# One of two transpose copies and the row sums go from ScalarE to VectorE (gated attention and a two-layer local-attention block on 8 cores)

## The chip, the cores and the metric

The kernel runs on all 8 cores of one Trainium2 chip. Each core takes one batch element (2048 x 1024) and all weights; the cores exchange nothing. The time is device microseconds of the slowest core. A core's engines are called PE (TensorE), ACT (ScalarE), DVE (VectorE), POOL (GpSimd) and SP (SyncE).

## The reference, cut to what matters

```python
xn = layernorm(x)
# gated attention; its softmax runs over the features D
q, k = silu(normed @ W_qk + b_qk) * gamma[0] + beta[0], ... * gamma[1] + beta[1]
sim  = einsum('bid,biD->bdD', q, k) / seq_len
attn = softmax(sim, axis=-1)
out  = v * sum(attn, axis=-1)[:, None, :]      # a row sum of a softmax
s    = (out * gate) @ W_out + b_out + xn
# two layers of local attention (8 heads of 64, window 512, one window back) and FFN
sim  = einsum('bhwid,bhwjd->bhwij', bq, bk)    # masked to a band of 512 back
attn = softmax(sim, axis=-1)
o    = einsum('bhwij,bhwjd->bhwid', attn, bv)
x    = x + o @ wo ;  x = x + ffn(x)
return x0 + s * silu(x)
```

## The kernel before

The program is a list of tasks written in order. `Prog.task` puts a task at the end of its engine's queue and works out from the names it reads and writes which semaphores it waits for; an engine runs its queue strictly in the order in which the tasks were written. `flush` closes a stage: all engines meet there, and the next stage's loads and products start behind it. The stages are: transposed layer norm, the QK projection, the similarity stage (`attn_p2`), the gated values and output (`attn_p34`), then for each of two layers QKV, local attention (`_local_attn`), the output projection, layer norm and FFN, and at last the final product.

**Similarity stage** (`attn_p2`, lines 563 to 644). The 2048 rows of `sim` are made in 16 blocks of 128 (`dt`), two for each of 8 query tiles `QT2` (called QT in the trace). For a query tile DVE makes 16 pieces with two instructions each (L588, L593). For a block PE makes 64 products of 512 columns into one half of `psim` (L605), DVE takes the row maximum (L614) and scales it (L618), ACT takes the exponential into `EB` with its sum in `small` (L623), DVE takes the reciprocal of this sum (L629), and ACT passes over `EB` once more, scaled by the reciprocal, with the sum of the result as `rowsum` (L633). Nothing but the sum is read later. In DVE's queue the next query tile stands behind the reciprocal of the pair's second block.

**Local attention** (`_local_attn`, from L1301). Two heads are worked on together (u = 0 and 1, the halves of the partitions), in 4 pairs `hp`, 4 windows `w` of 512 queries, and 4 steps `it` of 128 queries: 16 windows and 64 steps per layer. In a window w > 0 a step sees a band of 640 keys ("full band"), in w = 0 of 128, 256, 384 and 512. A step is:
- scores into `pS[u]` (L1329) and on top of them the mask as a product with the identity (L1336), for both u;
- then, of the step before, the transposes of `PB` into `pPT[u]` (L1396), and the copy of `pPT[u]` to `PT` (L1404, on ACT), both u;
- the softmax: negated row maxima of both u (L1350, DVE), exponentials of both u from `pS` into `PB` with their sums (L1358, ACT), reciprocals (L1367, DVE), and the scaling of `PB` (L1374, DVE).

The scores of the next step write `pS[u]`, so they wait for this step's exponential of the same u. Behind the fourth step come its own transposes and copies, and then the output product over all of `PT` (L1440), which ACT moves to `OA` (L1450). The order is the one of this loop:

```python
for it in range(4):
    for u in range(2):
        s_task(hp, w, it, u, jt0, iv)
    if it > 0:
        emit_tp(hp, w, it - 1)
    softmax(hp, w, it)
emit_tp(hp, w, 3)
```

`pPT` has a bank of PSUM for each u, and `pS` two. For V, DVE copies transposes out of a bf16 PSUM tile in the QKV stage (L865, `tensor_copy`).

Of the kernel before, what the change touches and what calls it, by code (L numbers as in the profile page):

```python
# [9 lines left out]
BF16 = mybir.dt.bfloat16  # L10
AF = mybir.ActivationFunctionType
ALU = mybir.AluOpType
# [5 lines left out]
HIDDEN, QKD = 2048, 2048  # L18
# [236 lines left out]
class Build:  # L255
# [307 lines left out]
    def attn_p2(self):  # L563
        nc, p, h = self.nc, self.p, self.h
        QK, GBC = self.QK, self.GBC
        gbc_res = tuple(f"GBC{r}.{c}" for r in range(4) for c in range(4))
        small = self.small
        with ExitStack() as S2:
            KF = S2.enter_context(nc.sbuf_tensor("KF", [128, NT, QKD], BF16))
            QT2 = S2.enter_context(nc.sbuf_tensor("QT2", [128, 2, NT, 256], BF16))  # L570
            EB = S2.enter_context(nc.sbuf_tensor("EB", [128, 2, QKD], BF16))
            psim = S2.enter_context(nc.psum_tensor("psim", [128, 2, QKD], F32))

            for t in range(NT):
                p.task("vector", lambda e, t=t: e.tensor_tensor(
                    KF[:, t, :], QK[:, t, :], GBC[:, 2, :], op=ALU.mult),
                    reads=(f"QK{t}.0", f"QK{t}.1", f"QK{t}.2", f"QK{t}.3")
                    + gbc_res,
                    writes=(f"KF{t}",), tag=f"p2.km{t}")
                p.task("vector", lambda e, t=t: e.tensor_tensor(  # L580
                    KF[:, t, :], KF[:, t, :], GBC[:, 3, :], op=ALU.add),
                    reads=(f"KF{t}",), writes=(f"KF{t}",), tag=f"p2.ka{t}")
            kf_res = tuple(f"KF{t}" for t in range(NT))

            for dp in range(8):
                qp = dp % 2
                for kt in range(NT):
                    p.task("vector", lambda e, dp=dp, kt=kt, qp=qp: e.tensor_tensor(  # L588
                        QT2[:, qp, kt, :], QK[:, kt, dp * 256:(dp + 1) * 256],
                        GBC[:, 0, dp * 256:(dp + 1) * 256], op=ALU.mult),  # L590
                        reads=(f"QK{kt}.{dp // 2}",) + gbc_res,
                        writes=(f"QT2{qp}.{kt}",), tag=f"p2.qm{dp}.{kt}")
                    p.task("vector", lambda e, dp=dp, kt=kt, qp=qp: e.tensor_tensor(  # L593
                        QT2[:, qp, kt, :], QT2[:, qp, kt, :],
                        GBC[:, 1, dp * 256:(dp + 1) * 256], op=ALU.add),
                        reads=(f"QT2{qp}.{kt}",), writes=(f"QT2{qp}.{kt}",),
                        tag=f"p2.qa{dp}.{kt}")
                qt_res = tuple(f"QT2{qp}.{kt}" for kt in range(NT))
                for dt in range(dp * 2, dp * 2 + 2):
                    pb = dt % 2  # L600
                    dl = (dt % 2) * 128
                    def simmm(e, dt=dt, pb=pb, dl=dl, qp=qp):
                        for c in range(4):
                            for kt in range(NT):
                                mm = e.matmul(  # L605
                                    psim[:, pb, c * 512:(c + 1) * 512],
                                    QT2[:, qp, kt, dl:dl + 128],
                                    KF[:, kt, c * 512:(c + 1) * 512],
                                    start=(kt == 0), stop=(kt == NT - 1))
                        return mm  # L610
                    p.task("tensor", simmm, reads=qt_res + kf_res,
                           writes=(f"psim{pb}",), tag=f"p2.sim{dt}")
                    sb = pb * 4
                    p.task("vector", lambda e, pb=pb, sb=sb: e.tensor_reduce(  # L614
                        small[:, sb:sb + 1], psim[:, pb, :], axis=AX.X, op=ALU.max),
                        reads=(f"psim{pb}",), writes=(f"p2max{pb}",),
                        tag=f"p2.max{dt}")
                    p.task("vector", lambda e, sb=sb: e.tensor_scalar(  # L618
                        small[:, sb + 1:sb + 2], small[:, sb:sb + 1], -1.0 / N,
                        None, op0=ALU.mult),  # L620
                        reads=(f"p2max{pb}",), writes=(f"p2bias{pb}",),
                        tag=f"p2.b{dt}")
                    p.task("scalar", lambda e, pb=pb, sb=sb: e.activation(  # L623
                        EB[:, pb, :], psim[:, pb, :], AF.Exp,
                        bias=small[:, sb + 1:sb + 2], scale=1.0 / N,
                        accum_out=small[:, sb + 2:sb + 3]),
                        reads=(f"psim{pb}", f"p2bias{pb}"),
                        writes=(f"EB{pb}", f"p2z{pb}"), tag=f"p2.exp{dt}")
                    p.task("vector", lambda e, sb=sb: e.reciprocal(  # L629
                        small[:, sb + 3:sb + 4], small[:, sb + 2:sb + 3]),  # L630
                        reads=(f"p2z{pb}",), writes=(f"p2rz{pb}",),
                        tag=f"p2.rz{dt}")
                    p.task("scalar", lambda e, dt=dt, pb=pb, sb=sb: e.activation(  # L633
                        EB[:, pb, :], EB[:, pb, :], AF.Identity,
                        scale=small[:, sb + 3:sb + 4],
                        accum_out=self.rowsum[:, dt:dt + 1]),
                        reads=(f"EB{pb}", f"p2rz{pb}"),
                        writes=(f"EB{pb}", f"rowsum{dt}"), tag=f"p2.rs{dt}")
            if "dbg_rowsum" in self.dbg_h:
                p.dma("sync", self.dbg_h["dbg_rowsum"][:], self.rowsum[:],  # L640
                      reads=tuple(f"rowsum{dt}" for dt in range(NT)),
                      writes=("dbg_rowsum.0",), tag="dbg.rowsum")
                self.out_res.append("dbg_rowsum.0")
            p.flush("p2")
# [656 lines left out]
    def _local_attn(self, l, QP, KP, VTM, OA, PB, PT, pS, pPT, pO):  # L1301
        p = self.p
        small = self.small
# [4 lines left out]
        def band(w, it):  # L1308
            if w == 0:
                return 0, (it + 1) * 128  # L1310
            return it * 128, 640
# [76 lines left out]
        def emit_tp(hp, w, it):  # L1388
            jlo, W = band(w, it)
            jb0 = jlo // 128  # L1390
            nb = W // 128
            for u in range(2):
                def ptp(e, u=u, it=it, jb0=jb0, nb=nb):
                    for jj in range(nb):
                        jb = jb0 + jj
                        mm = e.transpose(  # L1396
                            pPT[:, u, jj * 128:(jj + 1) * 128],
                            PB[:, it % 2, u, jb * 128:(jb + 1) * 128],
                            self.ident_bf[:])
                    return mm  # L1400
                p.task("tensor", ptp, reads=(f"PB{u}.{it % 2}", "identity_bf"),
                       writes=(f"pPT{u}",), tag=f"f{l}.tp{hp}.{w}.{it}.{u}")
                def pev(e, u=u, it=it, jb0=jb0, nb=nb):
                    return e.activation(  # L1404
                        PT[:, u, jb0:jb0 + nb, it * 128:(it + 1) * 128],
                        pPT[:, u, 0:nb * 128].rearrange("p (a b) -> p a b", b=128),
                        AF.Identity)
                p.task("scalar", pev, reads=(f"pPT{u}",),
                       writes=(f"PTc{u}.{it}",),
                       tag=f"f{l}.pe{hp}.{w}.{it}.{u}")  # L1410

        def icols(w, jt, njt):
            if w == 0:
# [5 lines left out]
        for hp in range(4):  # L1419
            for w in range(NW):  # L1420
                jt0 = 0 if w == 0 else (w - 1) * 4
                njt = 4 if w == 0 else 8
                for it in range(4):
                    iv = w * 512 + it * 128
# [6 lines that stand above are left out]
                pt_res = tuple(f"PTc{u}.{it}" for u in range(2) for it in range(4))  # L1431
                pbo = w % 2
                jt_order = list(range(njt)) if w == 0 else [3, 4, 2, 5, 1, 6, 0, 7]
                def omm(e, hp=hp, w=w, jt0=jt0, pbo=pbo, jt_order=jt_order):
                    for u in range(2):
# [13 lines left out]
                       writes=(f"pO{pbo}",), tag=f"f{l}.O{hp}.{w}")  # L1449
# [3 lines left out]
                    reads=(f"pO{pbo}",), writes=(f"OA{hp}.{w}",),  # L1453
                    tag=f"f{l}.Oe{hp}.{w}")
# [73 lines left out]
```

How the kernel before makes its waits and increments, by code:

```python
                    def _(eng):  # L114
                        cov = self.cov[e]
                        for (deps, emit, dslot, tag) in tasks:
                            for key, val in sorted(deps.items()):
                                if cov.get(key, 0) >= val:
                                    continue
                                if key[0] == "d":
                                    sem = self.dsems[key[1]][key[2]]
                                else:
                                    sem = self.sems[key[1]]
                                eng.wait_ge(sem, val)
                                cov[key] = val
                            if emit is None:
                                continue
                            if dslot is not None:
                                insts = emit(eng)
                                assert len(insts) == 1, tag
                                insts[0].then_inc(self.dsems[e][dslot], 16)
                            else:
                                inst = emit(eng)
                                if inst is None:
                                    inst = eng.nop()
                                inst.then_inc(self.sems[e], 1)
```

## Time and profile before

| | us |
|---|---|
| median of 2 runs | 4052.85 |
| the two runs | 3993.53 and 4112.18 |
| the profiled execution | 4013.77 |
| its span on the slowest core (core 1) | 4012.1 |
| spans of the other cores | 3970.2 to 3998.7 |

Busy over the span: PE 2726.5 us (68%), DVE 1149.4 (29%), ACT 916.6 (23%), POOL 203.9 (5%). Local attention of layer 0 lies at about 1537 to 1898 us, that of layer 1 at 2880 to 3236, the similarity stage at 442 to 791. The rows further down are of three kinds: groups of instructions with their mean duration and the idle time ahead of them; the timeline, where each row is a run of like instructions on one engine, with the idle time of the engine ahead of it and who ended it in brackets; and busy time by stage. In the timeline the start comes first and then the length, which for "x2" is from the first's start to the second's end.

### The profile page before, as it was taken

Reading aid. Unit: us, or ns where it says so; the run is one execution under the profiler, and the core shown is the slowest. Engines: PE = TensorE matmul, PEld = TensorE weight load, DVE = VectorE, ACT = ScalarE, POOL = GpSimd, SP = SyncE. Lnnn points to the kernel's source line nnn. Section 1 sums busy time; section 2 is a strip of 40 time slices with the busy share of each in tenths; the row PEclk is TensorE's granted clock in tenths of the full one; section 3 lists DMA queues with packets and bytes.
Section 4 is the critical chain, followed back from the end, with each engine's and each line's share of the span. In section 5 each row is a group of like instructions: output and inputs, shape, how many; then the busy total and the mean of one; then the engine's idle time right before and its main releaser. Section 6 shows DMA issues by size and latency. Waiting matters only on the chain. (4 is left out here: it accounts for less than half of the span.)

```text
span 4012.1 us, 34877 instructions; the slowest of 8 cores (3970.2 to 4012.1 us)
## 1 busy us (share of the span) xinstructions
PE 2726.5 (68%) x11952; PEld 1166.5 (29%) x11952; DVE 1149.4 (29%) x2109; ACT 916.6 (23%) x1570; POOL 203.9 (5%) x262
## 2 busy tenths in 40 slices
PE   1289476559693556655679898855665656989982
PEld 1223132224241113333123333311233322433432
DVE  3510523201012344443511111234444353111113
ACT  2322022123211213454021011021245412101101
POOL 0000000000000000000010111100000000111110
PEclk8577788879896766555789999966655577999995
DMA  5200000040344100000045555501000003565557
GB/s 125 80 6 1 0 0 0 15 70 1 58 130 128 21 11 11 1 1 5 7 53 63 58 68 62 65 11 21 11 1 1 1 11 37 69 61 60 63 59 251
DMA packets 213603, 170.26 MB, mean 42 GB/s; under 512 B 97573, under 2 KB 193976, under 8 KB 208312
## 3 DMA queue, kind: packets, MB, share of 16 engines
q0 software_dynamic: 200896, 119.59, 21.2%
q1 hardware_dynamic: 12536, 48.44, 4.1%
q8 instruction: 101, 1.65, 0.2%
q14 instruction: 70, 0.57, 0.1%
HBM read 237.26 MB, written 25.17 MB: 65 GB/s over the span
## 5 line engine op out<-in xcount | busy, mean ns | idle before, releaser
L1208 PE MATMUL pa<-N,W1B 128*128 128x512 bf16 x1408 | 339.1, 384 | 68.7 <-DMA W1B<-w1ag 68.7
L1170 PE MATMUL px<-PROD,W2B 128*128 128x512 bf16 x1408 | 324.0, 387 | 49.2 <-DMA W2B<-w2cb 49.0
L605 PE MATMUL psim<-KF,QT 128*128 128x512 bf16 x1024 | 236.2, 395 | 154.5 <-DVE QT L593 154.5
L1220 PE MATMUL pg<-N,W1B 128*128 128x512 bf16 x1408 | 336.2, 382 | 0.0
L1232 DVE TENSOR_TENSOR PROD<-pa,GEB 128x1024 bf16<-128x1024 f32 x88 | 107.8, 1225 | 630.9 <-ACT GEB L1227 630.9
L1329 PE MATMUL pS<-KP,QP 64*128 64x512 bf16 (+2 forms) x448 | 153.3, 426 | 162.1 <-ACT PB L1358 129.2
L889 PE MATMUL pqkv<-ABF,WQKV 128*128 128x512 bf16 x768 | 204.3, 432 | 64.8 <-DVE ESC L836 47.7
L1350 DVE TENSOR_REDUCE small<-pS 128x1 f32<-128x640 f32 (+4 forms) x256 | 183.3, 737 | 189.8 <-PE pS L1336 185.0
L1227 ACT ACTIVATE GEB<-pg,B1G 128x1024 bf16<-128x1024 f32 x88 | 98.1, 1115 | 553.9 <-PE pg L1220 553.9
L1396 PE MATMUL pPT<-ident_bf,PB 128*128 128x128 bf16 x1120 | 144.2, 311 | 99.1 <-DVE PB L1374 99.1
L1208 PEld LDWEIGHTS pa<-N,W1B 128*128 128x128 bf16 x1408 | 138.4, 99 | 240.1 <-issue 79.3
L1404 ACT ACTIVATE PT<-pPT 128x640 bf16<-128x640 bf16 (+4 forms) x256 | 149.8, 635 | 229.7 <-PE pPT L1396 229.2
L1170 PEld LDWEIGHTS px<-PROD,W2B 128*128 128x128 bf16 x1408 | 134.8, 99 | 222.8 <-issue 76.9
L1358 ACT ACTIVATE PB<-pS,small 128x640 bf16<-128x640 f32 (+4 forms) x256 | 184.8, 734 | 30.3 <-PE pS L1336 16.3
L605 PEld LDWEIGHTS psim<-KF,QT 128*128 128x128 bf16 x1024 | 102.9, 101 | 287.6 <-issue 176.6
L1220 PEld LDWEIGHTS pg<-N,W1B 128*128 128x128 bf16 x1408 | 123.6, 98 | 166.6 <-issue 43.1
L670 PE MATMUL pv<-ABF,WH 128*128 128x512 bf16 x512 | 122.5, 383 | 63.0 <-DMA WH<-W_hidden 63.0
L1396 PEld LDWEIGHTS pPT<-ident_bf,PB 128*128 128x128 bf16 x1120 | 120.2, 147 | 106.9 <-issue 106.6
L544 PE MATMUL pqk<-WQK,ABF 128*128 128x512 bf16 x512 | 147.5, 441 | 0.0
L1183 DVE TENSOR_TENSOR XF<-XF,px 128x512 f32<-128x512 f32 x64 | 44.0, 688 | 338.5 <-PE px L1173 338.5
L736 PE MATMUL ps<-VG,WO 128*128 128x512 bf16 x512 | 112.8, 384 | 39.0 <-DMA WO<-W_out 39.0
L889 PEld LDWEIGHTS pqkv<-ABF,WQKV 128*128 128x128 bf16 x768 | 82.8, 109 | 182.9 <-issue 117.6
(140 smaller groups left out, 2822.0 us busy)
## 6 DMA issues: line engine op xcount, KB each, us to landing
W1B<-w1ag POOLq DMA_DIRECT2D x88, 512.0 KB, 6.0
W2B<-w2cb POOLq DMA_DIRECT2D x32, 704.0 KB, 8.3
XT<-x SPq DMA_DIRECT2D x16, 512.0 KB, 4.2
xn_scr<-XNW POOLq DMA_DIRECT2D x16, 512.0 KB, 3.8
WH<-W_hidden POOLq DMA_DIRECT2D x8, 1024.0 KB, 32.0
XNB<-xn_scr SPq DMA_DIRECT2D x8, 1024.0 KB, 6.5
s_scr<-SB POOLq DMA_DIRECT2D x8, 1024.0 KB, 8.6
XF<-xn_scr SPq DMA_DIRECT2D x8, 1024.0 KB, 23.6
```

Source lines behind the costliest of these rows:

```text
L544: e.matmul(pqk[:, pb, :], ABF[:, k, t * 128:(t + 1) * 128], WQK[:, k, c * 512:(c + 1) * 512], start=(k == 0), stop=False)
L605: mm = e.matmul(psim[:, pb, c * 512:(c + 1) * 512], QT2[:, qp, kt, dl:dl + 128], KF[:, kt, c * 512:(c + 1) * 512], start=(kt == 0), stop=( ...
L670: mm = e.matmul(pv[:, sc, :], WH[:, k, hp * 128:(hp + 1) * 128], ABF[:, k, c * 512:(c + 1) * 512], start=(k == 0), stop=(k == DT - 1))
L889: mm = e.matmul(pqkv[:, sc, :], WQKV[:, k, ms * 128:(ms + 1) * 128], ABF[:, k, c * 512:(c + 1) * 512], start=(k == 0), stop=(k == DT - 1))
L1170: e.matmul(px[:, pb, :], W2B[:, s2, k, :], PROD[:, k, cc * 512:(cc + 1) * 512], start=(k == 0), stop=False)
L1208: e.matmul(pa[:, mp, cc * 512:(cc + 1) * 512], W1B[:, sl, k, 0:128], self.N2[:, k, nh0 + cc * 512:nh0 + (cc + 1) * 512], start=(k == 0), s ...
L1220: mm = e.matmul(pg2[:, mp, cc * 512:(cc + 1) * 512], W1B[:, sl, k, 128:256], self.N2[:, k, nh0 + cc * 512:nh0 + (cc + 1) * 512], start=(k ...
L1329: e.matmul(pS[:, u, lo:lo + n], QP[u * 64:(u + 1) * 64, hp, iv:iv + 128], KP[u * 64:(u + 1) * 64, hp, jt0 * 128 + lo:jt0 * 128 + lo + n], ...
L1350: p.task("vector", lambda e, u=u, sc=sc, jlo=jlo, W=W: e.tensor_reduce(small[:, sc:sc + 1], pS[:, u, jlo:jlo + W], axis=AX.X, op=ALU.max, ...
L1358: e.activation(PB[:, it % 2, u, jlo:jlo + W], pS[:, u, jlo:jlo + W], AF.Exp, bias=small[:, sc:sc + 1], accum_out=small[:, sc + 1:sc + 2]),
L1396: mm = e.transpose(pPT[:, u, jj * 128:(jj + 1) * 128], PB[:, it % 2, u, jb * 128:(jb + 1) * 128], self.ident_bf[:])
L1404: return e.activation(PT[:, u, jb0:jb0 + nb, it * 128:(it + 1) * 128], pPT[:, u, 0:nb * 128].rearrange("p (a b) -> p a b", b=128), AF.Iden ...
```

## The change

In the similarity stage the second pass of ACT over `EB` goes; in its place DVE multiplies the sum by its reciprocal, one number a partition. `EB` is now one tile and not two. In local attention the copy of u = 1 out of `pPT` is a `tensor_scalar` with 1.0 on DVE; the copy of u = 0 stays on ACT. The copies stay where they stood in the program, in `emit_tp`.

```diff
-            EB = S2.enter_context(nc.sbuf_tensor("EB", [128, 2, QKD], BF16))
+            EB = S2.enter_context(nc.sbuf_tensor("EB", [128, QKD], BF16))
...
-                    p.task("scalar", lambda e, dt=dt, pb=pb, sb=sb: e.activation(
-                        EB[:, pb, :], EB[:, pb, :], AF.Identity,
-                        scale=small[:, sb + 3:sb + 4],
-                        accum_out=self.rowsum[:, dt:dt + 1]),
-                        reads=(f"EB{pb}", f"p2rz{pb}"),
-                        writes=(f"EB{pb}", f"rowsum{dt}"), tag=f"p2.rs{dt}")
+                    p.task("vector", lambda e, dt=dt, sb=sb: e.tensor_tensor(
+                        self.rowsum[:, dt:dt + 1], small[:, sb + 2:sb + 3],
+                        small[:, sb + 3:sb + 4], op=ALU.mult),
+                        reads=(f"p2z{pb}", f"p2rz{pb}"),
+                        writes=(f"rowsum{dt}",), tag=f"p2.rs{dt}")
...
+                if u == 0:
...
+                    p.task("scalar", pev, reads=(f"pPT{u}",),
...
+                else:
+                    def pev(e, u=u, it=it, jb0=jb0, nb=nb):
+                        return e.tensor_scalar(
+                            PT[:, u, jb0:jb0 + nb, it * 128:(it + 1) * 128],
+                            pPT[:, u, 0:nb * 128].rearrange("p (a b) -> p a b",
+                                                            b=128),
+                            1.0, None, op0=ALU.mult)
+                    p.task("vector", pev, reads=(f"pPT{u}",),
+                           writes=(f"PTc{u}.{it}",),
+                           tag=f"f{l}.pe{hp}.{w}.{it}.{u}")
```

DVE's queue in local attention, full-band windows of layer 0, before (L1350 maxima, L1367 reciprocals, L1374 scaling of `PB`; "waits" names the semaphores that an instruction waits for):

```order
L1350 TENSOR_REDUCE small<-pS 128x1 [waits sem_tensor] x2
L1367 RECIPROCAL small<-small 128x1 [waits sem_scalar] x2
L1374 TENSOR_SCALAR PB<-PB,small 128x640 [waits sem_vector] x2
L1350 TENSOR_REDUCE small<-pS 128x1 [waits sem_tensor] x2
L1367 RECIPROCAL small<-small 128x1 [waits sem_scalar] x2
L1374 TENSOR_SCALAR PB<-PB,small 128x640 [waits sem_vector] x2
```

And now, from the start of a window (the lines are one less than before up to here, and L1414 is the copy of u = 1):

```order
L1349 TENSOR_REDUCE small<-pS 128x1 [waits sem_tensor] x2
L1366 RECIPROCAL small<-small 128x1 [waits sem_scalar] x2
L1373 TENSOR_SCALAR PB<-PB,small 128x640 [waits sem_vector] x2
L1414 TENSOR_SCALAR PT<-pPT 128x5x128 [waits sem_tensor]
L1349 TENSOR_REDUCE small<-pS 128x1 x2
L1366 RECIPROCAL small<-small 128x1 [waits sem_scalar] x2
L1373 TENSOR_SCALAR PB<-PB,small 128x640 [waits sem_vector] x2
L1414 TENSOR_SCALAR PT<-pPT 128x5x128 [waits sem_tensor]
```

A copy stands between the scaling of one step and the maxima of the next. It waits for PE; the maxima behind it have no wait of their own left, since the transposes stand behind their scores on PE.

DVE's queue in the similarity stage, before, where a pair of blocks ends and the next query tile begins:

```order
L618 TENSOR_SCALAR small<-small 128x1 [waits sem_vector]
L629 RECIPROCAL small<-small 128x1 [waits sem_scalar]
L588 TENSOR_TENSOR QT<-QK,GBC 128x256
L593 TENSOR_TENSOR QT<-QT,GBC 128x256 [waits sem_vector]
L588 TENSOR_TENSOR QT<-QK,GBC 128x256
```

And now:

```order
L618 TENSOR_SCALAR small<-small 128x1 [waits sem_vector]
L629 RECIPROCAL small<-small 128x1 [waits sem_scalar]
L633 TENSOR_TENSOR rowsum<-small 128x1 [waits sem_vector]
L588 TENSOR_TENSOR QT<-QK,GBC 128x256
L593 TENSOR_TENSOR QT<-QT,GBC 128x256 [waits sem_vector]
```

The row sum (L633) stands between the reciprocal and the next query tile, and waits for the reciprocal.

## Rows read from the trace of the kernel before

**Rows 1.** The page, its first line

```profile
span 4012.1 us, 34877 instructions; the slowest of 8 cores (3970.2 to 4012.1 us)
```

**Rows 2.** Busy time by stage (from:to, length, busy us per engine, granted clock)

```profile
1537.00:1898.00 361.00, 217.72 (x1220) 114.79 (x1221) 146.10 (x384) 178.59 (x400) 0.00 (x0) 0.53 0.01 3
...
442.00:791.00 349.00, 236.19 (x1024) 102.93 (x1024) 97.25 (x273) 67.76 (x65) 0.18 (x1) 0.85 0.00 0
```

**Rows 3.** Groups of instructions, shapes apart (| busy us, mean ns | idle before, releaser)

```profile
L1350 DVE TENSOR_REDUCE small<-pS 128x1 f32<-128x640 f32 x192 | 152.2, 820 | 142.5 <-PE pS L1336 140.2 <-issue 0.6
...
L1440 PE MATMUL pO<-PT,VTM 128*64 128x512 bf16 x112 | 55.4, 626 | 31.6 <-ACT PT L1404 31.6
```

**Rows 4.** Timeline, one step of a full-band window (start us, us, engine line)

```profile
1611.74 0.69 PE L1329 MATMUL pS<-KP,QP 64*128 64x256 bf16 x2 [1.89 <-ACT PB L1358]
...
1613.07 1.59 DVE L1350 TENSOR_REDUCE small<-pS 128x1 f32<-128x640 f32 x2
...
1613.52 1.27 PE L1396 MATMUL pPT<-ident_bf,PB 128*128 128x128 bf16 x10
...
1614.35 1.30 ACT L1404 ACTIVATE PT<-pPT 128x640 bf16<-128x640 bf16 x2 [2.09 <-PE pPT L1396]
...
1615.54 0.80 ACT L1358 ACTIVATE PB<-pS,small 128x640 bf16<-128x640 f32 x1
...
1616.68 0.69 PE L1329 MATMUL pS<-KP,QP 64*128 64x128 bf16 x2 [1.89 <-ACT PB L1358]
```

**Rows 5.** Timeline, first step of another window

```profile
1644.87 0.40 PE L1336 MATMUL pS<-MSK,ident_bf 128*128 128x128 bf16 x2
...
1645.37 1.80 DVE L1350 TENSOR_REDUCE small<-pS 128x1 f32<-128x640 f32 x2 [4.16 <-PE pS L1336]
...
1646.29 0.80 ACT L1358 ACTIVATE PB<-pS,small 128x640 bf16<-128x640 f32 x1 [1.30 <-PE pS L1336]
```

**Rows 6.** Groups of instructions of DVE, shapes apart, and one pair in the timeline

```profile
L1350 DVE TENSOR_REDUCE small<-pS 128x1 f32<-128x384 f32 x16 | 8.9, 555 | 0.8
...
L865 DVE COPY VTM<-ptv 128x512 bf16<-128x512 bf16 x32 | 12.0, 417 | 3.4 <-PE ptv L855 3.4
...
L1374 DVE TENSOR_SCALAR PB<-PB,small 128x640 bf16<-128x640 bf16 x192 | 65.6, 383 | 0.8 <-DVE small L1367 0.6
...
1512.98 0.74 DVE L865 COPY VTM<-ptv 128x512 bf16<-128x512 bf16 x2
```

**Rows 7.** Timeline, end of a full-band window

```profile
1622.89 1.23 PE L1396 MATMUL pPT<-ident_bf,PB 128*128 128x128 bf16 x10 [3.15 <-DVE PB L1374]
...
1623.68 1.30 ACT L1404 ACTIVATE PT<-pPT 128x640 bf16<-128x640 bf16 x2 [1.52 <-PE pPT L1396]
...
1625.12 3.81 PE L1440 MATMUL pO<-PT,VTM 128*64 128x512 bf16 x16 [1.01 <-ACT PT L1404]
```

**Rows 8.** Timeline, middle step of a first window (w = 0)

```profile
1634.21 0.63 PE L1396 MATMUL pPT<-ident_bf,PB 128*128 128x128 bf16 x4
...
1635.27 0.59 ACT L1358 ACTIVATE PB<-pS,small 128x384 bf16<-128x384 f32 x1
```

**Rows 9.** Timeline, similarity stage, a pair of blocks and the stage ends

```profile
521.41 0.16 DVE L629 RECIPROCAL small<-small 128x1 f32<-128x1 f32 x1 [2.25 <-ACT EB L623]
...
521.49 0.27 DVE L588 TENSOR_TENSOR QT<-QK,GBC 128x256 bf16<-128x256 bf16 x1
...
521.87 0.29 DVE L593 TENSOR_TENSOR QT<-QT,GBC 128x256 bf16<-128x256 bf16 x1
...
788.00 2.00 ACT L633 ACTIVATE EB<-EB,small 128x2048 bf16<-128x2048 bf16 x1 [0.36 <-DVE small L629]
...
789.90 0.19 ACT L633 ACTIVATION_READ_ACCUMULATOR EB<-EB,small 128x1 f32 x1
...
790.82 4.29 POOL L94 DMA_DIRECT2D WH<-W_hidden  x8 [578.63 <-SPq L106]
```

**Rows 10.** Timeline, output product of another full-band window

```profile
1600.75 3.29 PE L1440 MATMUL pO<-PT,VTM 128*64 128x512 bf16 x16 [1.01 <-ACT PT L1404]
```

More of the change, by code:

```diff
@@ L623, in attn_p2 @@
                     p.task("scalar", lambda e, pb=pb, sb=sb: e.activation(
-                        EB[:, pb, :], psim[:, pb, :], AF.Exp,
+                        EB[:, :], psim[:, pb, :], AF.Exp,
                         bias=small[:, sb + 1:sb + 2], scale=1.0 / N,
@@ L627, in attn_p2 @@
                         reads=(f"psim{pb}", f"p2bias{pb}"),
-                        writes=(f"EB{pb}", f"p2z{pb}"), tag=f"p2.exp{dt}")
+                        writes=("EB0", f"p2z{pb}"), tag=f"p2.exp{dt}")
                     p.task("vector", lambda e, sb=sb: e.reciprocal(
@@ L1402, in emit_tp, with pev @@
                        writes=(f"pPT{u}",), tag=f"f{l}.tp{hp}.{w}.{it}.{u}")
[L1403 to L1410, printed above, removed]
+                if u == 0:
+                    def pev(e, u=u, it=it, jb0=jb0, nb=nb):
+                        return e.activation(
+                            PT[:, u, jb0:jb0 + nb, it * 128:(it + 1) * 128],
+                            pPT[:, u, 0:nb * 128].rearrange("p (a b) -> p a b",
+                                                            b=128),
+                            AF.Identity)
+                    p.task("scalar", pev, reads=(f"pPT{u}",),
+                           writes=(f"PTc{u}.{it}",),
+                           tag=f"f{l}.pe{hp}.{w}.{it}.{u}")
+                else:
+                    def pev(e, u=u, it=it, jb0=jb0, nb=nb):
+                        return e.tensor_scalar(
+                            PT[:, u, jb0:jb0 + nb, it * 128:(it + 1) * 128],
+                            pPT[:, u, 0:nb * 128].rearrange("p (a b) -> p a b",
+                                                            b=128),
+                            1.0, None, op0=ALU.mult)
+                    p.task("vector", pev, reads=(f"pPT{u}",),
+                           writes=(f"PTc{u}.{it}",),
+                           tag=f"f{l}.pe{hp}.{w}.{it}.{u}")
         def icols(w, jt, njt):
```

## The prediction, made before the changed kernel ran

> **What bounds the kernel now.** I began with the span [rows 1]: 4012.1 us on the slowest core in an execution of 4013.77 us, so 1.7 us lie around it. The sum below is made against 4013.77. The median of the two runs shown is 4052.85 us, 1% above it, and the two lie 119 us apart (3993.53 and 4112.18); a time near the upper one would have to be read with that in mind.
>
> Then busy time by stage [rows 2]. The diff touches the similarity stage once (about 349 us) and the local attention of both layers (about 360 us each). In local attention no engine is full: PE is busy 218 of 361 us, DVE 146, ACT 179, at a granted clock of 0.53, which is near the lower of the two levels (1.2 GHz). A stage in which nothing is full and the clock is low is bound by a chain of waits that goes round between engines. So what counts is not how much work an engine has, but what stands in front of the instruction that the chain passes through.
>
> The groups [rows 3] say where the waits are: DVE waits 142.5 us ahead of the row maxima (L1350), almost all for PE; the output product (L1440) waits 31.6 us for ACT's copies of the transposes (L1404), about 1 us in each of the 32 windows.
>
> The timeline of one step of the loop over `it` [rows 4] shows the round. At 1611.74 PE starts the scores of the next step, goes on with their mask products, and then transposes ten blocks of the present step, until 1613.52 + 1.27 = 1614.79. Meanwhile DVE has scaled PB and taken both maxima, 1613.07 to 1614.66, before the transposes are even done. ACT copies both halves (u=0, u=1) from 1614.35, and both exponentials come right behind: the first at 1615.54. The next scores can start only when it has emptied its half of pS: at 1616.68. One round is 4.94 us, and from the first exponential to the next scores are 1.14 us of it. The maxima are not on this round: they are over nearly a microsecond before the exponential starts.
>
> **Local attention: the copy of u=1 goes from ACT to DVE.** 128 copies leave ACT and 128 `tensor_scalar` come to DVE; 96 on each side have 640 columns. By work alone this is a gain: ACT is on the round, and it gets rid of one copy of some 0.65 us.
>
> But the order on DVE (see the change above) puts the copy of step it-1 ahead of both maxima of step it. It waits for the last transpose, which PE issues behind the scores of step it. So the maxima, which now run before and beside the transposes, must wait for them, and behind the maxima stand both exponentials, and the next scores behind the first exponential. The wait is long and its place is on the round. The new start of the first exponential is:
> - end of the transposes, 1614.79 [rows 4];
> - to the start of DVE's copy 0.10: a step's first mask products end at 1644.87 + 0.40 = 1645.27 and the maximum starts at 1645.37 [rows 5];
> - from the copy's start to the maximum's, d (below);
> - from the maximum's start to the exponential's 0.92, as 1645.37 to 1646.29, where nothing else held it [rows 5].
>
> With d = 0 this is already 1615.81, 0.27 later than the 1615.54 of today. Three such steps are 0.81 us, and all that a window's end can give back is less (0.76, below), so by this working there is no gain whatever the copy's speed.
>
> **The size of d.** The trace has no `tensor_scalar` from a bf16 tile in PSUM. Nearest is L865, DVE's copy from a bf16 PSUM tile in blocks of 128 with the same form of output: 417 ns for 512 columns, and two in 0.74 us, so 0.74 - 0.42 = 0.32 from start to start [rows 6]. The f32 maximum of L1350 takes 820 ns for 640 and 555 for 384 columns, 1.04 ns a column [rows 3, 6]; L865 spends less than that, and half of it per column (0.52) adds 0.07 for the other 128. So d = 0.39 and the copy is 0.48 long. Below: L1374 scales 640 bf16 columns in SBUF in 0.38, and with an overlap of 0.08, between the maxima's and L865's, d = 0.30 [rows 6]. Above: the rate of the f32 maxima, which are 0.82 long, two in 1.59, so d = 0.77 [rows 3, 4]. I take 0.39, since L865 differs least.
>
> The Trainium skill, in "VectorE: DVE Perf Modes", section "Rules for kernel authors", tells one to accept 1x for elementwise work on a matmul's output; by that the upper end, 0.77, would be the value. L865 is against it here, with 417 ns for 512 columns; I keep it as a rival.
>
> **Per window.** With d = 0.39 the first exponential starts at 1614.79 + 0.10 + 0.39 + 0.92 = 1616.20, so 0.66 late. The second needs the second maximum, 0.77 behind the first, and ACT spaces the exponentials 0.83 apart anyway, so it isn't later than that. All of this enters the round: 4.94 becomes 5.60. It happens in steps 1, 2 and 3 of a window (in step 0 the maxima stand behind the previous window's last copy, but they have to wait for the scores behind the output product anyway): 3 x 0.66 = 1.98.
>
> At the window's end something comes back. The last transposes end at 1622.89 + 1.23 = 1624.12 and ACT's copies of both halves run 1623.68 to 1624.98; the output product starts at 1625.12 [rows 7]. Now the halves run side by side, and DVE's ends at 1624.12 + 0.10 + 0.48 = 1624.70: 0.28 earlier (a copy of no length would give 1624.98 - 1624.22 = 0.76). Net 1.98 - 0.28 = 1.70 us in each of the 24 windows of full band: 40.8.
>
> The 8 first windows (w = 0) have bands of 128 to 512 columns. Middle step: transposes end 1634.21 + 0.63 = 1634.84, a copy of 256 columns gives d = 0.19 by the same rate, and the maximum of 384 columns to its exponential takes 0.55 + 0.10, so 1635.78 against 1635.27: 0.51 late [rows 8]. Three such and 0.2 back at the end (my estimate, from the 0.28 of a full band): 1.3 x 8 = 10.6. Both together: +51.4 us.
>
> With d = 0.30: 3 x 0.57 less 0.38 at the end = 1.33 x 24 = 32, and with 10 for the first windows +42. With d = 0.77: 3 x 1.04, and at the end DVE is 0.06 later than ACT was, so 3.18 x 24 = 76; the first windows' steps rise by some 0.18 each and lose their 0.2, so 2.1 x 8 = 17: +93.
>
> **Similarity stage: the row sum.** ACT's 16 passes over EB (2.0 us each) go; 16 products of 128x1 come to DVE. ACT is busy 68 of 349 us there [rows 2], and no instruction of the trace waits for these passes. Fifteen of the passes lie beside score products or DVE's query tiles, so removing them gives nothing. Only the last counts, as its accumulator is read at 789.90 + 0.19 = 790.09 and the next stage's weight loads leave behind it, at 790.82 [rows 9]. Its successor on DVE starts 0.11 behind the reciprocal (a dependent pair of DVE: 521.49 + 0.27 to 521.87), at 788.01, and is over by about 788.2: 1.9 us gained. Against that, the query tiles start 0.08 behind the reciprocal's start today (521.41 to 521.49) [rows 9] and PE waits for them; now a dependent product stands between, 0.16 + 0.11 = 0.27 more, in 7 places: 1.9 lost. Net 0; bounds -2 (nothing lost) and +2 (0.5 a place). The smaller EB frees room that nothing uses.
>
> **Sum.** 4013.8 + 51.4 + 0 = 4065, so +1.3%. A measurement of this kernel can tell about 2% (80 us) from no change; by this the forecast is "within 2%", on the slow side of it.
>
> **Rivals.**
> - *The copy runs at the rate of the f32 maxima* (d = 0.77): 4013.8 + 93 = 4107, slower by 2.3%. This is the case on the other side of the mark; the place is the wait of L1350 in the 96 steps; it decides when the copy of 640 columns takes over 0.74 us (42 us come with 0.38 more of d, so the 80 us are reached at d = 0.65). For it: the f32 reads of PSUM in rows 3 and 6 run so. Against: L865.
> - *The clock.* The output product of a full-band window takes 3.29 us or 3.81 [rows 7, 10]; I read this as the clock going to its upper level earlier or later in it. If PE, idler now, lost this in all 24 windows, and the scores behind it lost as much again (my estimate), 24 x 2 x 0.52 = 25 us would come on top: 4090, 1.9%. For it: the clock is 0.53 already. Against: it rises during the output product, which doesn't change.
> - *The freed copy is what counts.* If the maxima weren't late, the exponential would start one copy earlier: 0.65 in 72 steps, half of that (my estimate) in the 24 narrow ones, and 8 us at the windows' ends, 63 in all: 3951, faster by 1.6%. The Trainium skill, "ScalarE: Activation LUTs", section "Rules for kernel authors", is for it: multiplications belong on VectorE rather than on ScalarE; the trace agrees as to length (L865 and L1404, 0.48 by my estimate against some 0.65). Against the rival is the order: the maxima can't pass the copy.
> - *Nothing moves*, 4014: the late exponentials would have to be paid by a wait between them and the next scores. The trace has no such wait in the 1.14 us that lie there.
>
> **Chances.** Forecast 0.70; f32 rate 0.13; clock 0.08; freed copy 0.04; nothing 0.05. The second lies over 2%, and half of the clock case, which is 4 us short of it: slower 0.17. Faster by 2% needs more than any case gives: 0.02; within: 0.81. The range: low end 4013.8 + 42, less the 20 us by which the faster run shown lies under the profiled one, 4036; high end the second case's 4107 and 20 for the same, 4127.
>
> **What would show it.** Right: in a full-band step L1350 starts behind DVE's copy and ACT waits ahead of L1358 for L1350's maximum; the round is 5.5 to 5.7 us; the copy row reads 0.45 to 0.50; local attention is 25 us longer per layer; the output product waits for ACT or DVE 0.7 us a window. The similarity stage keeps its length within 2 us. Wrong: a round of 4.94 or less, or exponentials that start right behind ACT's copy, or a copy row of 0.8.

## The result, and the profile after

The changed kernel is slower by 1.4%: the ratio is 1.0138, with a 95% interval of [1.0093, 1.0182]. Its median over 11 runs is 4060.16 us. The median of the kernel before over all its 10 runs is 4076.46 us, above this, because medians count disturbed executions too, which the ratio leaves out on both sides. The profiled execution took 4045.38 us, against 4013.77 before. The two profiles differ by less than 1.4%, since on the core that was the slowest before (and on one other) the score products of the similarity stage began some 25 us later than on most others (442.4 against about 416 us), ahead of everything that the change touches; stage lengths, further down, are free of this.

The page's first lines, core 2, the slowest:

```profile
span 4043.4 us, 34668 instructions; the slowest of 8 cores (4031.8 to 4043.5 us)
...
PE 2698.1 (67%) x11952; PEld 1162.5 (29%) x11952; DVE 1204.4 (30%) x2253; ACT 824.7 (20%) x1410; POOL 203.9 (5%) x262
```

ACT has lost 92 us of work and DVE has gained 55, and the kernel is longer. Busy time of local attention in layer 0 (from:to, length, busy us of PE, PEld, DVE, ACT and POOL, granted clock), as in [rows 2]; it takes 386 us where it took 361:

```profile
1512.00:1898.00 386.00, 216.04 (x1216) 113.86 (x1216) 171.95 (x448) 149.79 (x336) 0.00 (x0) 0.54 0.01 3
```

The groups, as in [rows 3] (busy us, mean ns, idle before and its releasers):

```profile
L1357 ACT ACTIVATE PB<-pS,small 128x640 bf16<-128x640 f32 x192 | 151.1, 791 | 114.8 <-DVE small L1349 96.1 <-PE pS L1335 16.9 <-DVE small L1366 0.5
L1349 DVE TENSOR_REDUCE small<-pS 128x1 f32<-128x640 f32 x192 | 149.8, 815 | 99.6 <-PE pS L1335 97.8
...
L1404 ACT ACTIVATE PT<-pPT 128x640 bf16<-128x640 bf16 x96 | 67.6, 704 | 181.1 <-PE pPT L1395 181.1
...
L1414 DVE TENSOR_SCALAR PT<-pPT 128x640 bf16<-128x640 bf16 x96 | 47.2, 491 | 147.9 <-PE pPT L1395 147.9
...
L1451 PE MATMUL pO<-PT,VTM 128*64 128x512 bf16 x112 | 55.4, 626 | 23.7 <-DVE PT L1414 23.7
```

DVE's reciprocals, before and after:

```profile
L1367 DVE RECIPROCAL small<-small 128x1 f32<-128x1 f32 x256 | 41.9, 164 | 237.2 <-ACT PB L1358 235.8
```

```profile
L1366 DVE RECIPROCAL small<-small 128x1 f32<-128x1 f32 x256 | 42.0, 164 | 118.8 <-ACT PB L1357 117.5
```

Three entries tell the story. Ahead of the exponentials (L1357) ACT now waits 96.1 us for DVE's maxima. The new copy (L1414) waits 147.9 us for the transposes. And DVE's wait for the exponentials, ahead of its reciprocals, has fallen from 237.2 to 118.8 us: where it used to take both maxima first and then wait, it now waits for the transposes first, and the maxima are late by it. The wait that stands in the row of the maxima itself (142.5 us before, 99.6 now) isn't the sign of the loss: 140.0 of the 142.5 us and 97.2 of the 99.6 lie in the first steps of the windows, ahead of the first maximum. The copy itself takes 491 ns.

One step of a full-band window in the timeline, the counterpart of [rows 4]:

```profile
1593.13 0.69 PE L1328 MATMUL pS<-KP,QP 64*128 64x256 bf16 x2 [2.56 <-ACT PB L1357]
...
1594.91 1.27 PE L1395 MATMUL pPT<-ident_bf,PB 128*128 128x128 bf16 x10
1595.75 0.70 ACT L1404 ACTIVATE PT<-pPT 128x640 bf16<-128x640 bf16 x1 [2.09 <-PE pPT L1395]
1596.30 0.49 DVE L1414 TENSOR_SCALAR PT<-pPT 128x640 bf16<-128x640 bf16 x1 [1.75 <-PE pPT L1395]
1596.70 1.54 DVE L1349 TENSOR_REDUCE small<-pS 128x1 f32<-128x640 f32 x2
1597.61 0.79 ACT L1357 ACTIVATE PB<-pS,small 128x640 bf16<-128x640 f32 x1 [1.16 <-DVE small L1349]
...
1598.75 0.69 PE L1328 MATMUL pS<-KP,QP 64*128 64x128 bf16 x2 [2.56 <-ACT PB L1357]
```

The round is 1598.75 - 1593.13 = 5.62 us, where it was 4.94. The reader should go down the starts: transposes end at 1594.91 + 1.27 = 1596.18, the copy starts 0.12 behind, the first maximum 0.40 behind that, the exponential 0.91 behind that, the next scores 1.14 behind that. ACT has been done with its own copy since 1596.45 and idles 1.16 us until the maximum is there.

The end of a window, as in [rows 7], with both copies side by side and PE's wait at 0.75 us, which was 1.01:

```profile
1605.86 1.22 PE L1395 MATMUL pPT<-ident_bf,PB 128*128 128x128 bf16 x10 [4.06 <-DVE PB L1373]
1606.65 0.70 ACT L1404 ACTIVATE PT<-pPT 128x640 bf16<-128x640 bf16 x1 [1.52 <-PE pPT L1395]
1607.19 0.49 DVE L1414 TENSOR_SCALAR PT<-pPT 128x640 bf16<-128x640 bf16 x1 [1.18 <-PE pPT L1395]
...
1607.83 3.81 PE L1451 MATMUL pO<-PT,VTM 128*64 128x512 bf16 x16 [0.75 <-DVE PT L1414]
```

The middle step of a first window, as in [rows 8]:

```profile
1520.13 0.63 PE L1395 MATMUL pPT<-ident_bf,PB 128*128 128x128 bf16 x4
...
1520.88 0.29 DVE L1414 TENSOR_SCALAR PT<-pPT 128x256 bf16<-128x256 bf16 x1 [1.10 <-PE pPT L1395]
...
1521.72 0.58 ACT L1357 ACTIVATE PB<-pS,small 128x384 bf16<-128x384 f32 x1 [0.69 <-DVE small L1349]
```

From the transposes' end (1520.76) to the exponential are 0.96 us, where it was 0.43. In the similarity stage, as in [rows 9], first a pair's end, then the stage's end, and last the reciprocal that began the stage's end in the kernel before:

```profile
495.94 0.16 DVE L629 RECIPROCAL small<-small 128x1 f32<-128x1 f32 x1 [2.25 <-ACT EB L623]
496.21 0.16 DVE L633 TENSOR_TENSOR rowsum<-small 128x1 f32<-128x1 f32 x1
496.29 0.29 DVE L588 TENSOR_TENSOR QT<-QK,GBC 128x256 bf16<-128x256 bf16 x1
```

```profile
762.77 0.16 DVE L629 RECIPROCAL small<-small 128x1 f32<-128x1 f32 x1 [2.25 <-ACT EB L623]
763.03 0.16 DVE L633 TENSOR_TENSOR rowsum<-small 128x1 f32<-128x1 f32 x1
763.94 4.29 POOL L94 DMA_DIRECT2D WH<-W_hidden  x8 [551.38 <-SPq L106]
```

```profile
787.74 0.16 DVE L629 RECIPROCAL small<-small 128x1 f32<-128x1 f32 x1 [2.26 <-ACT EB L623]
```

From the reciprocal's start to the query tile's are 0.35 us, which was 0.08; from the last reciprocal's start to the weight loads 1.17, which was 790.82 - 787.74 = 3.08.

A measure that the late start of two cores doesn't touch is the time from the first row maximum of layer 0 to the start of the last eviction of the output product of layer 1 on each core, with all that lies between. Its median over the eight cores is used below as "the attention stretch". It is 1690.1 us before and 1745.1 after: 55.0 us longer, 1.4% of the whole. The score products of the similarity stage, from the first start to the last and again as a median, take 341.1 us before and 341.6 after (339.0 to 341.8 on the single cores before).

### The profile page after: what moved, and what is told of

It reads as the page before. It is cut to its first block and busy times, and to the rows that moved or that the text cites. A ratio compares the mean times of both kernels' runs of the same rounds, so it can differ in the third digit from the quotient of the medians.

```text
span 4043.4 us, 34668 instructions; the slowest of 8 cores (4031.8 to 4043.5 us)
## 1 busy us (share of the span) xinstructions
PE 2698.1 (67%) x11952; PEld 1162.5 (29%) x11952; DVE 1204.4 (30%) x2253; ACT 824.7 (20%) x1410; POOL 203.9 (5%) x262
## 5 line engine op out<-in xcount | busy, mean ns | idle before, releaser
L1357 ACT ACTIVATE PB<-pS,small 128x640 bf16<-128x640 f32 (+4 forms) x256 | 184.1, 723 | 133.5 <-DVE small L1349 113.5
L669 PE MATMUL pv<-ABF,WH 128*128 128x512 bf16 x512 | 122.6, 383 | 61.3 <-DMA WH<-W_hidden 61.3
L735 PE MATMUL ps<-VG,WO 128*128 128x512 bf16 x512 | 112.2, 383 | 40.8 <-DMA WO<-W_out 40.8
L1404 ACT ACTIVATE PT<-pPT 128x640 bf16<-128x640 bf16 (+4 forms) x128 | 81.5, 637 | 226.9 <-PE pPT L1395 226.9
L460 PE MATMUL pbf<-ident_bf,NTB 128*128 128x128 bf16 x128 | 16.2, 305 | 160.3 <-DVE NTB L452 160.3
```

Source lines behind the costliest of these rows:

```text
L669: mm = e.matmul(pv[:, sc, :], WH[:, k, hp * 128:(hp + 1) * 128], ABF[:, k, c * 512:(c + 1) * 512], start=(k == 0), stop=(k == DT - 1))
L735: mm = e.matmul(ps[:, pb, :], WO[:, k, mo * 128:(mo + 1) * 128], VG[:, k, c * 512:(c + 1) * 512], start=(k == 0), stop=(k == NT - 1))
L1357: e.activation(PB[:, it % 2, u, jlo:jlo + W], pS[:, u, jlo:jlo + W], AF.Exp, bias=small[:, sc:sc + 1], accum_out=small[:, sc + 1:sc + 2]),
```

## The experiments

The order theory was: the copy stands in DVE's queue ahead of the next step's maxima, so the maxima wait for the transposes, and the exponentials and the next scores for the maxima. Its main rival, the work theory: DVE has more to do, or reads PSUM beside ACT, and that costs wherever the copy stands.

**The copy behind the maxima.** From the changed kernel, the put of the u = 1 copy is held back until `softmax` has written its two maxima:

```diff
-                        emit_tp(hp, w, it - 1)
-                    softmax(hp, w, it)
+                        held = emit_tp(hp, w, it - 1, late=(1,))
+                    softmax(hp, w, it, held_mx=held)
```

> The changed kernel with one thing moved: DVE's copy of u=1 stands behind the two maxima of the next step and no longer ahead of them. Order theory (the loss comes from what stands in front of the maxima, not from the work): the first exponential of a full-band step starts right behind ACT's single copy, about 0.59 us earlier than in the kernel before, the round falls from 4.94 to about 4.35 us, and with 0.28 at each window's end some 58 us are gained: 0.986 of the kernel before. Work theory (DVE has more to do and reads PSUM beside ACT, wherever the copy stands): the round stays at 5.6 us and the ratio at 1.014.

Measured: ratio 0.9837, interval [0.9813, 0.9861]; the attention stretch is 1628.8 us, 61.3 shorter than before the change and 116 shorter than after it. The timeline of a full-band step:

```profile
1587.23 0.70 ACT L1409 ACTIVATE PT<-pPT 128x640 bf16<-128x640 bf16 x1 [2.09 <-PE pPT L1400]
1587.78 0.49 DVE L1424 TENSOR_SCALAR PT<-pPT 128x640 bf16<-128x640 bf16 x1 [0.24 <-PE pPT L1400]
1587.83 0.79 ACT L1359 ACTIVATE PB<-pS,small 128x640 bf16<-128x640 f32 x1
...
1592.18 0.79 ACT L1359 ACTIVATE PB<-pS,small 128x640 bf16<-128x640 f32 x1
```

The same 0.49 us copy now runs beside the exponential (1587.78 and 1587.83), which starts right behind ACT's single copy. The next step's exponential is at 1592.18, 4.35 us after 1587.83, as expected. The work theory falls: DVE has the same 2253 instructions (busy 1206.5 us, against 1204.4), and the sign of the result has turned.

**The halves exchanged.** DVE copies u = 0, ACT u = 1, in the changed kernel's places.

```diff
-                if u == 0:
+                if u == 1:
                     def pev(e, u=u, it=it, jb0=jb0, nb=nb):
                         return e.activation(
```

> The changed kernel with the halves exchanged: the copy of u=0 is DVE's, that of u=1 is ACT's, same places in the order. DVE has the same work, but its transposes end 0.54 us earlier. Order theory: the maxima start that much earlier, the round is about 5.1 us (4.94 + 0.14), the loss falls to some 16 us, ratio about 1.004. Work theory: ratio 1.014 as before, round 5.6.

Measured: 1.0031 [1.0004, 1.0058]; attention stretch 1710.1, 20.0 longer than before, where some 16 were expected.

```profile
1591.82 0.69 PE L1328 MATMUL pS<-KP,QP 64*128 64x256 bf16 x2 [2.03 <-ACT PB L1357]
...
1594.45 0.49 DVE L1414 TENSOR_SCALAR PT<-pPT 128x640 bf16<-128x640 bf16 x1 [1.22 <-PE pPT L1395]
1594.86 1.55 DVE L1349 TENSOR_REDUCE small<-pS 128x1 f32<-128x640 f32 x2
...
1595.77 0.80 ACT L1357 ACTIVATE PB<-pS,small 128x640 bf16<-128x640 f32 x1
...
1596.91 0.69 PE L1328 MATMUL pS<-KP,QP 64*128 64x128 bf16 x2 [2.03 <-ACT PB L1357]
```

The round is 5.09 us. DVE's copy and maxima are where they were in the queue, but their transposes are ready earlier, and some two thirds of the loss are gone. What is paid is the moment at which the copy can start, plus its length.

**The copy twice.** A second `tensor_scalar` into the same place behind the first (the output doesn't change by it).

```diff
                     p.task("vector", pev, reads=(f"pPT{u}",),
                            writes=(f"PTc{u}.{it}",),
                            tag=f"f{l}.pe{hp}.{w}.{it}.{u}")
+                    p.task("vector", pev, reads=(f"pPT{u}",),
+                           writes=(f"PTc{u}.{it}",),
+                           tag=f"f{l}.pf{hp}.{w}.{it}.{u}")
```

> The changed kernel with DVE's copy made twice into the same place. The second waits for the first, so the maxima start 0.49 + 0.11 = 0.60 us later. Order theory (the copy's whole length is on the round): round 5.61 + 0.60 = 6.2 us, 43 us more in full-band steps, 10 in the narrow ones and 18 at the windows' ends, together 71 us more than the changed kernel, some 1.031 of the kernel before. If the length of the copy were hidden and only the wait for the transposes counted, the round would stay at 5.6.

This run gave no ratio, only the profile. The step on core 4:

```profile
1596.83 0.79 ACT L1357 ACTIVATE PB<-pS,small 128x640 bf16<-128x640 f32 x1 [1.76 <-DVE small L1349]
...
1601.12 1.09 DVE L1414 TENSOR_SCALAR PT<-pPT 128x640 bf16<-128x640 bf16 x2 [1.75 <-PE pPT L1395]
1602.13 1.55 DVE L1349 TENSOR_REDUCE small<-pS 128x1 f32<-128x640 f32 x2
1603.04 0.79 ACT L1357 ACTIVATE PB<-pS,small 128x640 bf16<-128x640 f32 x1 [1.76 <-DVE small L1349]
```

From the copy's start to the first maximum are 1.01 us, where one copy makes it 0.40: 0.61 more. The exponential is at 1603.04, against 1596.83 a step earlier: a round of 6.21. The attention stretch is 1817.6, 72.5 longer than after the change (1816.0 and 70.9 by cores 4 to 7 alone), where 71 were expected. So the copy's length stands on the round in full, and d, the term that the prediction had to bound, enters the sum as it had it.

**The row sum alone.** Local attention is that of the kernel before, the similarity stage that of the changed one.

```diff
-                    p.task("scalar", lambda e, dt=dt, pb=pb, sb=sb: e.activation(
...
+                    p.task("vector", lambda e, dt=dt, sb=sb: e.tensor_tensor(
+                        self.rowsum[:, dt:dt + 1], small[:, sb + 2:sb + 3],
+                        small[:, sb + 3:sb + 4], op=ALU.mult),
...
```

> The kernel before with only the row sum moved to DVE (similarity stage), local attention untouched. My theory: 1.9 us gained at the stage's end and 0.27 in each of 7 places lost, ratio 1.000 within the interval; the first to the last score product of the stage take 0.27 x 7 = 2 us longer, and the following stage starts 2 us sooner behind the last of them. Rival: the missing ACT passes free something that I haven't seen, ratio below 0.995.

> The kernel with only the row sum moved, once more and with more rounds, since the first time gave no interval. My theory: 1.000, within 0.002 either way. Rival: the row sum gives some of the time that the first run hinted at (its two lowest executions lay 5 us below those of the kernel before), ratio 0.998 or less.

Neither run gave a ratio. What they show: the lowest of the first was 3986.06 us and that of the second 3994.80, beside 3991.71 and 3991.46 for the kernel before on the same chip at the same time; one lies below and one above. The score products' stretch was 340.3 and 341.4 us (341.1 before), the attention stretch 1685.8 and 1687.4 (1690.1 before). These are differences that two profiles of one kernel could show as well. The row sum is worth less than these runs can tell, within some 6 us either way; that it is exactly nothing isn't shown.

**The copy alone.** The other half: similarity stage as before, local attention as changed.

```diff
+                else:
+                    def pev(e, u=u, it=it, jb0=jb0, nb=nb):
+                        return e.tensor_scalar(
...
+                    p.task("vector", pev, reads=(f"pPT{u}",),
```

> The kernel before with only the copy of u=1 moved to DVE, at the place that the change gives it. My theory: the whole loss, ratio 1.013 to 1.015, first maximum to last eviction of OA 55 us longer than in the kernel before. Rival: part of the loss comes from the row sum, ratio 1.010 or less.

Measured: 1.0109 [1.0055, 1.0163], an interval too wide to tell 1.010 from 1.014; one execution of the kernel before, at 4039.14, widens it. The lowest of each, 4043.07 and 3991.46, make 1.0129. The attention stretch decides it: 1742.9 us, 52.8 longer than before, against 55.0 with both parts. The loss is the copy's; the 2.2 us between the two are hardly more than the 1.6 by which the two profiles of the row-sum kernel differ.

**Both copies behind maxima and exponentials.** If the place in the queue is what counts, more can be moved out of the round's way: ACT's copy needn't stand ahead of the exponentials either.

```diff
-                        emit_tp(hp, w, it - 1)
-                    softmax(hp, w, it)
+                        held = emit_tp(hp, w, it - 1, late=(0, 1))
+                    softmax(hp, w, it, held_ex=held)
```

> The changed kernel with both copies of a step written behind the maxima and exponentials of the next step: ACT runs its exponentials ahead of its copy of u=0, DVE its maxima ahead of its copy of u=1. The round then no longer goes through transposes and copies: scores to first maximum 1.3 us (DVE has just scaled PB), to the exponential 0.92, to the next scores 1.14, together about 3.4 us against 4.35 with the copy only behind the maxima, with PE's 3.05 us of work per step close below. Order theory: 1.54 x 72 us and some 17 in the narrow steps and 8 at the windows' ends come off the kernel before, 0.966; somewhat less if PE's clock rises with its busier stage. Work theory: DVE with 3.2 us of work per step, and waits on PE's queue, keeps the round above 4 us: 0.98 or more.

Measured: 0.9698 [0.967, 0.9726], median 3870.14 us; attention stretch 1567.4, 122.7 shorter than before.

```profile
1576.86 0.79 ACT L1359 ACTIVATE PB<-pS,small 128x640 bf16<-128x640 f32 x1 [1.12 <-DVE small L1349]
...
1578.42 0.70 ACT L1409 ACTIVATE PT<-pPT 128x640 bf16<-128x640 bf16 x1
...
1579.33 1.59 DVE L1349 TENSOR_REDUCE small<-pS 128x1 f32<-128x640 f32 x2
...
1579.78 1.27 PE L1400 MATMUL pPT<-ident_bf,PB 128*128 128x128 bf16 x10
1580.24 0.80 ACT L1359 ACTIVATE PB<-pS,small 128x640 bf16<-128x640 f32 x1 [1.12 <-DVE small L1349]
```

The exponential starts 0.91 us behind the maximum and 0.81 us ahead of the end of the transposes of the step before (1581.05). From 1576.86, the exponential one step earlier, to 1580.24 are 3.38 us, as expected. The stretch became 123 us shorter, where I had worked out 136. The first windows gave the 17 us expected (16.5); the full-band ones gave 107.6 of 119, and where the other 11 are wasn't traced.

**The same order with all copies on ACT.** The kernel before, not the changed one, with the same two lines.

> The kernel before (both copies on ACT, second pass over EB on ACT) with only the order changed: both copies of a step behind the maxima and exponentials of the next. Order theory: ACT's 3.0 us of work per step fit into a round of about 3.4 us, so nearly all of the gain comes without moving any work to DVE: 0.97. If it is the split of the copies that makes the gain and order only lets it through, the round stays above 4.3 us: 0.985 or more.

Measured: 0.9703 [0.9675, 0.9732], median 3873.66 us; attention stretch 1567.0.

```profile
1575.77 0.80 ACT L1360 ACTIVATE PB<-pS,small 128x640 bf16<-128x640 f32 x1 [0.53 <-DVE small L1350]
...
1577.32 1.30 ACT L1409 ACTIVATE PT<-pPT 128x640 bf16<-128x640 bf16 x2
...
1578.68 1.27 PE L1401 MATMUL pPT<-ident_bf,PB 128*128 128x128 bf16 x10
1579.15 0.80 ACT L1360 ACTIVATE PB<-pS,small 128x640 bf16<-128x640 f32 x1 [0.53 <-DVE small L1350]
```

ACT makes both copies (1.30 us) between one step's exponentials and the next, and the round is 1579.15 - 1575.77 = 3.38 us, the same as with the split. With the order right, moving a copy to DVE is worth nothing that can be told: 0.9703 and 0.9698. With the order as it was, the move costs 1.4%. (The split kernel has the row sum on DVE too, this one on ACT; the attention stretch leaves that stage out.) Both these kernels beat the kernel before by 3% and the changed one by more than 4%.

## Why the prediction was right, and where it was wrong

**The round.** Right in each link. Forecast and measured: to DVE's copy 0.10 and 0.12; d 0.39 and 0.40; maximum to exponential 0.92 and 0.91; round 5.60 and 5.62. The experiment with the copy twice shows that d counts in full, and the one with the copy behind the maxima that nothing but its place makes the loss.

**The size of d.** L865 was the right row to go by: the copy takes 491 ns where 0.48 us was taken. The Trainium skill's "VectorE: DVE Perf Modes", section "Why PSUM operands drop a tier", caps an operand in PSUM at 2x, and an fp32 one at 1x; the rows agree, as 128 more columns cost 67 ns from 512 (424 ns) to 640 (491 ns), half of the 1.04 ns a column of the f32 maxima. The rule for authors that I weighed in the forecast, to accept 1x, doesn't hold for this source, and the rival of a copy at the f32 rate (d = 0.77) is out.

**The windows.** A window's end gave back 0.26 (PE's wait 1.01 to 0.75) of the forecast 0.28. The narrow middle step lost 0.53 us where the forecast had 0.51. The sum is 55.0 us by the attention stretch against 51.4. Taken from eviction to eviction (medians over the cores), the 24 full-band windows together are 43.5 us longer (599.7 to 643.1), of which the measured links make (3 x 0.68 - 0.26) x 24 = 42.7 and the forecast made 40.8. The 8 first windows are 12.3 longer (123.6 to 135.9), where the forecast had 10.6.

**The row sum.** Both halves of the working came as forecast: 0.27 more ahead of a query tile (0.35 for 0.08) and 1.91 less at the stage's end (1.17 for 3.08). By this arithmetic they cancel. The 7 x 0.27 = 1.9 us that the score products should have lost don't show in their stretch, which grew by 0.5, within the scatter of the cores, and the two runs of this part alone show nothing that can be told.

**The clock.** The granted clock of local attention in layer 0 is 0.54 where it was 0.53, and all products of the output (four widths, 448) are busy 156.0 us where it was 154.2. The rival of a fallen clock is out. Its 25 us were too many besides: it took the clock to rise in all 24 windows, but of the two products in rows 7 and 10 only the second saw it rise (0.66 from 1602.00 to 1604.04, then 1.00); through the first, 1625.12 to 1628.93, it stood at 0.50.

**The freed copy.** The rival that fewer copies on ACT make the exponential early is what the copy behind the maxima shows: 0.9837. It was a true gain that this change's order kept from appearing; I gave it 63 us and it was worth 61.3, but in another kernel, and with 0.59 us a full-band step where I had 0.65.

**A row misread.** The prediction took the 142.5 us ahead of the maxima as where the waits are, and the rival of the f32 rate names this wait as its place "in the 96 steps". Nearly all of it (140.0) lies in the first steps of the windows; in the other three the maxima began without a wait before the change. No term of the sum rests on this row.

**What was wrong.** The sum, 4065 us or +1.3%, agrees with the measured median of 4060.16 and ratio of 1.0138, and the range held it. That the two absolute times lie only 5 us apart is partly luck: the base of the sum, 4013.77, lies 20 us above the fastest execution before (3993.53), and the median lies 12 above the fastest after (4047.73). The ratio, and the 54.2 us between the fastest two, are the fair comparison for the 51.4. The step that failed is the sentence behind the sum: "A measurement of this kernel can tell about 2% (80 us) from no change; by this the forecast is 'within 2%'". I let this mark stand for the forecast's answer, although my own working excluded a gain for every length of the copy, and put its lowest value at +42 us; by the mark 0.81 of the chances went to "within" and 0.17 to "slower". The measurement tells far less than 80 us apart: its interval is 0.45 points to each side, some 18 us, and it lies clear of 1. No row gave the 80 us; they were put down without a working. By my sum the change was a small and sure loss, and that is how it should have been called.

## What to carry to other kernels

Before work is moved to the engine with more idle time, look at what it will stand in front of in that engine's queue, and at when it can start: here a copy of 0.49 us cost 0.68 us of every full-band step behind a window's first, because the maxima behind it had to wait for its transposes as well. If a stage has no full engine and goes round between them, write down the links of one round with their starts, and move what the next link doesn't need (here both copies, whose result only the output product reads) behind what it does; this alone gave 3%, and the split that the change was about gave nothing on top.

A sum that excludes a gain at both its ends is a forecast of a loss, however small; a bound for what can be measured says how sure the answer will look, not which sign it has.

## What the runs showed that I had not expected

That the split is worth nothing that can be told once the order is right: 1567.4 against 1567.0 us for the attention stretch. I had expected some 8 us for the windows' ends. In the profile PE's waits ahead of the output product do add up to 7.1 us less with the split. First the kernel with the split, then the one with all copies on ACT:

```profile
L1468 PE MATMUL pO<-PT,VTM 128*64 128x512 bf16 x112 | 55.4, 626 | 23.4 <-DVE PT L1424 23.4
```

```profile
L1452 PE MATMUL pO<-PT,VTM 128*64 128x512 bf16 x112 | 55.4, 626 | 30.5 <-ACT PT L1409 30.5
```

The local attention of both layers, each from its first maximum to its last eviction, takes 599.1 us with the split and 601.7 without, but the cores of one kernel lie further apart than that (598.8 to 601.9, and 600.3 to 603.9). Where the rest of the 7 us is lost again wasn't tried.
